# Two routings of a mixture-of-experts kernel: first router's operands swapped, stores ahead of weights, bf16 tables relaid, lots of 18, 8 and 6 tiles

## The reference, cut to what matters

```
x: 16 sequences x 256 tokens x 128; 8 experts; hidden size 512
x = x + 0.5 * ffn(layernorm(x))
x = x + attention(layernorm(x))        # 16 heads of 8; q, k: rms norm, then rope
x = x + 0.5 * ffn(layernorm(x))        # the same weights

ffn(z): e = argmax(z @ Wr.T + br)      # one expert per token
        y = relu(z @ W1[e].T + b1[e]) @ W2[e].T + b2[e]
```

## Time and profile before

| | us |
|---|---|
| median of 3 runs | 552.09 (551.03 to 552.29) |
| profiled execution | 550.08 |
| its span, first to last instruction | 547.6 |
| PE / DVE / ACT / POOL busy | 477.7 / 385.6 / 339.2 / 288.6 |

### The profile page before, as it was taken

How to read it: one execution, slowest core, us unless ns; L and a number is a source line. 1 busy time by engine, 2 the same in 40 slices (tenths; PEclk the granted TensorE clock), 3 DMA queues, 4 the chain that set the end, 5 groups by cost and what they waited for, 6 DMA issues and landing times.

```text
span 547.6 us, 13826 instructions
## 1 busy us (share of the span) xinstructions
PE 477.7 (87%) x4184; PEld 344.8 (63%) x4187; DVE 385.6 (70%) x1044; ACT 339.2 (62%) x763; POOL 288.6 (53%) x407
## 2 busy tenths in 40 slices
PE   6958999999688899999999999998988269979991
PEld 6825999996244555555555555555554159869991
DVE  6194777773578688888988888878886048956760
ACT  2204667661353688888888888887766436546650
POOL 6005455432699577777675656664037704564442
PEclk9998999999895699999999999999997869998997
DMA  8971222211000000000000000000001122223100
GB/s 226 344 129 37 59 64 67 68 37 40 26 25 11 20 12 13 13 7 13 8 12 7 2 2 5 2 3 2 2 23 56 54 49 78 75 65 86 46 30 0
DMA packets 28566, 24.88 MB, mean 45 GB/s; under 512 B 5651, under 2 KB 26042, under 8 KB 28240
## 3 DMA queue, kind: packets, MB, share of 16 engines
q1 hardware_dynamic: 23952, 15.52, 10.6%
q0 software_dynamic: 4544, 8.49, 5.5%
HBM read 14.65 MB, written 9.99 MB: 45 GB/s over the span
## 4 chain that ended last, share of the span: by engine, by line
PE 65%; DVE 14%; issue 9%; ACT 4%; DMA 3%; POOL 2%; DVEq 1%; POOLq 0%; ACTq 0%; SPq 0%
PE PS L647 12%; PE PS L660 11%; PE PS L786 10%; PE PS L749 9%; DVE Smax L1422 6%; PE PS L734 5%; PE PS L719 4%; PE PS L596 2%; PE PS L771 2%; PE PS L816 2%; PE PS L796 1%; ACT QkT L871 1%; PE PS L589 1%; PE PS L637 1%; PE PS L759 1%
## 5 line engine op out<-in xcount | busy, mean ns | idle before, releaser
L1422 DVE TENSOR_REDUCE Smax<-PS 128x4 f32<-128x1024 f32 x128 | 156.1, 1223 | 39.5 <-PE PS L749 37.2
L967 ACT ACTIVATE Pt<-PS 128x1024 f32<-128x1024 f32 x128 | 128.4, 1033 | 4.8 <-PE PS L771 4.0
L647 PE MATMUL PS<-XsT,Ws 128*128 128x128 f32 x624 | 91.6, 291 | 2.0 <-ACT XsT L871 2.0
L660 PE MATMUL PS<-W,HsT 128*128 x624 | 84.8, 279 | 3.8 <-DVE Ys L1320 2.7
L910 ACT ACTIVATE HsT<-PS,Bs 128x128 f32<-128x128 f32 x156 | 48.7, 363 | 63.1 <-PE PS L647 57.9
L647 PEld LDWEIGHTS PS<-XsT,Ws 128*128 128x128 f32 x624 | 78.0, 196 | 7.2 <-ACT XsT L871 3.2
L660 PEld LDWEIGHTS PS<-W,HsT 128*128 128x128 f32 x624 | 76.9, 194 | 6.6 <-issue 6.4
L439 POOL DMA_INDIRECT Xs<-rows,TokI x39 | 39.1, 1001 | 70.0 <-DVE TokI L1275 34.9
L749 PE MATMUL PS<-QkT 24*128 24x256 f32 x512 | 64.5, 329 | 12.9 <-DVE Smax L1422 9.4
L749 PEld LDWEIGHTS PS<-QkT 24*128 24x128 f32 x512 | 40.8, 192 | 49.6 <-issue 17.8
L786 PE MATMUL PS<-Pt,Vg 128*32 128x256 f32 x1024 | 71.0, 396 | 0.1
(11 more groups left out here) (183 smaller groups left out, 735.2 us busy)
## 6 DMA issues: line engine op xcount, KB each, us to landing
AtCol<-slots SPq DMA_DIRECT2D x39, 65.5 KB, 1.8
mid<-Ys SPq DMA_DIRECT2D x39, 64.0 KB, 1.6
rows<-XX SPq DMA_DIRECT2D x8, 260.0 KB, 8.8
XX<-x SPq DMA_DIRECT2D x8, 256.0 KB, 4.5
W<-w1T SPq DMA_DIRECT2D x1, 2048.0 KB, 8.2
W<-w2T SPq DMA_DIRECT2D x1, 2048.0 KB, 13.1
QkT<-NmaxT SPq DMA_DIRECT2D x64, 4.0 KB
Xs<-rows,TokI POOLq DMA_INDIRECT x39
```

Source lines behind the costliest of these rows:

```text
L647: last = nc.tensor.matmul(PS[:, 2 + 2 * (n % 2) + c // 2, (c % 2) * P:(c % 2 + 1) * P], Ws[:, n % R_WS, c * P:(c + 1) * P], XsT[:, n % 2, ...
L660: last = nc.tensor.matmul(PS[:, y_bank(n), 0:P], HsT[:, n % 2, c, :], W2[:, ds(e * D_FF + c * P, P)], start=(c == 0), stop=(c == FC - 1))
L967: nc.scalar.activation(Pt[:, m % 2, 2 * pair:2 * pair + 2, :, :].rearrange("p h c t -> p (h c t)"), PS[:, score_bank(m, pair):score_bank(m ...
L1422: nc.vector.tensor_reduce(Smax[:, b % 2, :, at:at + 33:32].rearrange("p t h -> p h t"), PS[:, max_bank(m, pair):max_bank(m, pair) + 2, :]. ...
```

## The change

Router 1: `Wr32`, the centred weights in 32 columns, is now stationary and `XT` moves, 512 tokens at a time; four groups go to four strips of 32 partitions of one bank, ACT copies it (`logits_copy`), and PE turns it back (`turn_logits`). `XT` keeps all 8 groups, and all of them can be turned with three banks. PE starts with 8 filler matmuls. Row stores move ahead of W2, B2 and the attention weights on SP, with the wait for `ln_shift`; the semaphore `w_in` is split in three. The tables have the tile number innermost, their operands are bf16, and `ColAll` and `TileAll`, written by POOL, hold their counting side in full. `AtCol` is one operation, and `invert` starts behind it. B2's scaling stands behind `TokI`. Routing 2: lots of 18, 8 and 6 tiles instead of 16, 10 and 6, lot 0 in steps 47 to 51 instead of 52 to 55.

```diff
-ROUTE_LOTS = ((0, 16), (16, 26), (26, 32))
-POOL_NORM_AT = 44
+ROUTE_LOTS = ((0, 18), (18, 26), (26, 32))
+POOL_NORM_AT = 42
...
-HOT_AT = {52: 0, 57: 1}
+HOT_AT = {47: 0, 57: 1}
...
-PLACE_AT = {55: 0, 59: 1}
+PLACE_AT = {51: 0, 59: 1}
...
-        ModF = sb("ModF", [P, N_TILES])
+        ModF = sb("ModF", [P, N_TILES], BF16)
-        AtCol = sb("AtCol", [P, N_TILES, P], BF16)
-        AtTile = sb("AtTile", [P, N_TILES, S_TILES], BF16)
-        Ids = sb("Ids", [P, N_TILES, 2, S_TILES], BF16)
+        AtCol = sb("AtCol", [P, P, N_TILES], BF16)
+        AtTile = sb("AtTile", [P, S_TILES, N_TILES], BF16)
+        Ids = sb("Ids", [P, 2, S_TILES, N_TILES], BF16)
...
+        XT = Pt[:].rearrange("p u h c t -> p (u h c t)").rearrange("p (c x) -> p c x", c=N_CHUNK)
...
-        XT = Sq[:].rearrange("p u q t d -> p u (q t d)")
+        LgT = Sq[:].rearrange("p u q t d -> p u (q t d)")
...
+        ColAll = RotRn[:].rearrange("p a u q t d -> p (a u q t d)").bitcast(BF16).rearrange("p (c j) -> p c j", j=N_TILES)
...
+        TileAll = YuT[:].rearrange("p g t -> p (g t)").bitcast(BF16)[:, 0:S_TILES * N_TILES].rearrange("p (t j) -> p t j", j=N_TILES)
...
+        TURN_BANKS, LGT_BANKS, LG_BANKS = (0, 1, 4), (2, 3), (6, 5)
...
-            for dst, src in ((W1, w1T), (W2, w2T), (B2, b2.partition_broadcast(P)),
-                             (G8, g_rms.partition_broadcast(P)), (Cos, rope_cos), (Sin, rope_sin)):
-                sp.dma_start(dst[:], src).then_inc(w_in, 16)
...
+            sp.dma_start(W1[:], w1T).then_inc(w1_in, 16)
+            sp.wait_ge(ln_shift, 1)
+            for c in range(N_CHUNK):
+                a, b = c * CH, (c + 1) * CH
+                sp.dma_start(row_tiles[:, a:b, :], XX[:, a:b, 0:P + 2]).then_inc(rows_out[c], 16)
+            for dst, src in ((W2, w2T), (B2, b2.partition_broadcast(P))):
+                sp.dma_start(dst[:], src).then_inc(w2_in, 16)
+            for dst, src in ((G8, g_rms.partition_broadcast(P)), (Cos, rope_cos), (Sin, rope_sin)):
+                sp.dma_start(dst[:], src).then_inc(rope_in, 16)
...
                     sp.dma_start(Wp[at:at + HD, 0:P], wpT[HD * (GH * g + h):HD * (GH * g + h + 1), :]).then_inc(wp_in, 16)
-
-            sp.wait_ge(ln_shift, 1)
-            for c in range(N_CHUNK):
-                a, b = c * CH, (c + 1) * CH
-                sp.dma_start(row_tiles[:, a:b, :], XX[:, a:b, 0:P + 2]).then_inc(rows_out[c], 16)
...
-            nc.gpsimd.iota(TileCol[:], [[1, S_TILES]], channel_multiplier=0, allow_small_or_imprecise_dtypes=True).then_inc(const_done, 1)
+            nc.gpsimd.iota(TileAll, [[1, S_TILES], [0, N_TILES]], channel_multiplier=0, allow_small_or_imprecise_dtypes=True).then_inc(const_done, 1)
+            nc.gpsimd.iota(ColAll, [[1, P], [0, N_TILES]], channel_multiplier=0, allow_small_or_imprecise_dtypes=True).then_inc(const_done, 1)
...
-            def turn_chunk(c, bank):
+            def turn_chunk(c):
+                pe.wait_ge(x_in[c], 16)
+                if c >= len(TURN_BANKS):
+                    pe.wait_ge(xnT_ready, c - len(TURN_BANKS) + 1)
                 for u in range(CH):
-                    last = nc.tensor.transpose(PS[:, bank, u * P:(u + 1) * P], X[:, CH * c + u, :], I[:])
+                    last = nc.tensor.transpose(PS[:, TURN_BANKS[c % len(TURN_BANKS)], u * P:(u + 1) * P], X[:, CH * c + u, :], I[:])
                 last.then_inc(xnT_ps, 1)
 
-            def logits(c, bank):
-                pe.wait_ge(xnT_ready, c + 1)
+            def logits(r):
+
+                pe.wait_ge(xnT_ready, CH * (r + 1))
+                for i in range(CH):
+                    last = nc.tensor.matmul(PS[32 * i:32 * i + 32, LGT_BANKS[r], :], Wr32[:], XT[:, CH * r + i, :],
+                                            start=True, stop=True)
+                last.then_inc(lgT_ps, 1)
+
+            def turn_logits(r):
+                pe.wait_ge(lgT_ready, r + 1)
                 for u in range(CH):
-                    j = CH * c + u
-                    last = nc.tensor.matmul(PS[:, bank, j * N_EXP:(j + 1) * N_EXP],
-                                            XT[:, c % 2, u * P:(u + 1) * P], WrC,
-                                            start=True, stop=True)
+                    last = nc.tensor.transpose(PS[:, LG_BANKS[r], u * P:(u + 1) * P], LgT[:, r, u * P:(u + 1) * P], I[:])
                 last.then_inc(logits_ps, 1)
...
                 pe.wait_ge(ids_ready, 2)
+                pe.wait_ge(at_col, 1)
                 for j in range(N_TILES):
-                    if j % (N_TILES // 2) == 0:
-                        pe.wait_ge(at_col, 2 * j // N_TILES + 1)
-                    last = nc.tensor.matmul(PS[:, 3, 0:2 * S_TILES], AtCol[:, j, :],
-                                            Ids[:, j, :, :].rearrange("p a t -> p (a t)"),
+                    last = nc.tensor.matmul(PS[:, 3, 0:2 * S_TILES], AtCol[:, :, j],
+                                            Ids[:, :, :, j].rearrange("p a t -> p (a t)"),
                                             start=(j == 0), stop=(j == N_TILES - 1))
...
+            pe.wait_ge(const_done, 1)
+            fill_const(8)
             pe.wait_ge(turn_in, 16 * 2)
             pe.wait_ge(unit_ready, 1)
             nc.tensor.matmul(PS[:, 5, 0:N_EXP], Unit[:], Wr[:], start=True, stop=True).then_inc(wr_sum, 1)
-            pe.wait_ge(const_done, 1)
-            for c in range(N_CHUNK + 1):
-                if c < N_CHUNK:
-                    pe.wait_ge(x_in[c], 16)
-                    if c >= 2:
-                        pe.wait_ge(xnT_ready, c - 1)
-                    turn_chunk(c, c % 2)
-                if c == 1:
-                    pe.wait_ge(wr_centred, 1)
-                if c >= 1:
-                    logits(c - 1, 2)
+            for c in range(6):
+                turn_chunk(c)
+                if c < 4:
+                    fill_const(1)
+            pe.wait_ge(wr_centred, 1)
+            logits(0)
+            turn_chunk(6)
+            turn_chunk(7)
+            turn_logits(0)
+            logits(1)
...
-            fill_const(8)
+            turn_logits(1)
+            fill_const(14)
             totals()
-            fill_const(20)
+            fill_const(22)
             invert()
-            fill_const(14)
-            pe.wait_ge(w_in, 16 * 8)
+            fill_const(18)
+            pe.wait_ge(w2_in, 16 * 2)
             experts(0)
...
-                    nc.tensor.matmul(PS[:, 5, :], AtCol[:, 0, :], AtCol[:, 0:4, :].rearrange("p j d -> p (j d)"),
+                    nc.tensor.matmul(PS[:, 5, :], Col[:], Col[:].unsqueeze(1).to_broadcast([P, 4, P]),
...
-            for c in range(N_CHUNK):
-                if c == N_CHUNK // 2:
-                    inverse_deviation(0)
-                chunk_copy(c, c % 2)
+            for c in range(6):
+                chunk_copy(c)
+            logits_copy(0)
+            for c in range(6, N_CHUNK):
+                chunk_copy(c)
+            logits_copy(1)
+            inverse_deviation(0)
...
-                dve.wait_ge(logits_ps, N_CHUNK)
+                for r in range(2):
+                    half = slice(r * N_TILES // 2, (r + 1) * N_TILES // 2)
+                    dve.wait_ge(logits_ps, r + 1)
+                    last = tt_(Lg[:, half].rearrange("p (i u) e -> p u i e", u=CH),
+                               PS[:, LG_BANKS[r], :].rearrange("p (u i x) -> p u i x", u=CH, i=CH)[:, :, :, 0:N_EXP],
+                               Rstd[:, half].rearrange("p (i u) -> p u i", u=CH).unsqueeze(3).to_broadcast([P, CH, CH, N_EXP]),
+                               ALU.mult)
                 dve.wait_ge(route_in, 16 * 5)
-                scaled_logits(every, PS[:, 2, 0:N_TILES * N_EXP].rearrange("p (j e) -> p j e", e=N_EXP))
+                link(last)
+                link(tt_(Lg[:], Lg[:], Br[:].unsqueeze(1).to_broadcast([P, N_TILES, N_EXP]), ALU.add))
...
-                wide = [P, N_TILES, S_TILES]
-                tt_(AtTile[:], TileCol[:].unsqueeze(1).to_broadcast(wide),
-                    DivF[:].unsqueeze(2).to_broadcast(wide), ALU.is_equal).then_inc(at_tile, 1)
+                wide = [P, S_TILES, N_TILES]
+                tt_(AtTile[:], TileAll, DivF[:].unsqueeze(1).to_broadcast(wide), ALU.is_equal).then_inc(at_tile, 1)
                 dve.wait_ge(at_tile, 1)
-                tt_(Ids[:, :, 0, :], AtTile[:], FromEnd[:].unsqueeze(2).to_broadcast(wide), ALU.mult).then_inc(ids_ready, 1)
-                for a in range(0, N_TILES, N_TILES // 2):
-                    b = a + N_TILES // 2
-                    wide = [P, N_TILES // 2, P]
-                    tt_(AtCol[:, a:b, :], Col[:].unsqueeze(1).to_broadcast(wide),
-                        ModF[:, a:b].unsqueeze(2).to_broadcast(wide), ALU.is_equal).then_inc(at_col, 1)
+                tt_(Ids[:, 0, :, :], AtTile[:], FromEnd[:].unsqueeze(1).to_broadcast(wide), ALU.mult).then_inc(ids_ready, 1)
```

(17 more changed lines are left out.)

47 lines of the change are left out of this document (27 added, 20 removed).

## The result

On the chip of the first comparison the kernel after took 544.5 us (median of 11 runs, 541.4 to 559.7) and the kernel before beside it 552.3: 0.986 of it, 95% interval 0.983 to 0.989. That is 7.8 us faster, where I had forecast 22.6; 544.5 lies above my range. The profiled execution took 547.41 us, span 545.6.

The account below looks back on a forecast made before the run. Bounds: the router (0 to 47 us; PE, then DVE alone) and 11.00 us of issue between attention and second experts. Router -11.4 and second routing -11.2 made -22.6: profiled 550.08 to 527.5, median 529.5 us; range 521 to 539.

Parts of the forecast that it names:

- Logit group: Router, sign to look for: PE's logit group takes 1.1 us, not 1.9.
- the rival of a clock that never rises: Router: PE stays at half clock, +5.8 us, 535.3 in all; chance 0.20.
- AtTile 0.81 and AtCol 2.29: Router tables: bf16, innermost-dense operands bring AtTile near 0.8 and AtCol near 2.3; tables together -3.4 us.
- the second half of the router's product: Router: DVE's product, now two halves, ends at 16.1 instead of 25.40, -9.3 us.
- the seam's arithmetic: Between attention and second expert stage: last store issued by 426.6, first Xr at 430.9 instead of 441.27, -10.4 us.
- DVE's routing work of lot 0: Second routing: 4.0 us of work moved into attention steps 47 to 51 lengthens attention by +1.2 us.
- W2 and B2 at 404 GB/s: Router loads: queued behind row stores ending at 27.2, they land at 33.7, in time for Xr; +0.5 us booked.
- 32 matmuls behind it instead of 16: Router inversion: waiting for the whole AtCol costs +1.2 us, ends 0.6 and 3.6.
- the lesser case: Router rival: 64-byte steps make the inversion cost double, +2.4 us; chance 0.10 together with tables not speeding up.
- After the idle 11 us: Start of second expert stage: without idle time PE keeps full clock, -2 us, ends 0 and -2.5.
- the router's 11.4: Router's summed gain at the first Xr: -9.3 - 3.4 + 1.2 - 0.4 + 0.5 = -11.4 us.
- 11.2: Second routing's summed gain: seam -10.4, DVE work +1.2, clock -2, together -11.2 us.

Follow-up runs that it names:

- scans_first: Kernel after with lot 0's scans at the head of step 49, ahead of the normalisation: 537.8 us, 0.976 of the kernel before.
- warm: scans_first with 36 instead of 22 filler matmuls ahead of the inversion and 40 instead of 18 behind: 571.3 us (0.998); on another chip 565.0 (0.994).
- tiles_outer: scans_first with the first routing's tables in the old layout, tiles outermost and columns contiguous: 574.4 us, 1.008 of the kernel before.
- parts 2 to 5: Follow-up experiments on four other chips, with variants of the kernels before and after; the kernel before took 569.7, 567.7, 566.8 and 570.1 us there.

## Why the prediction was wrong

**Right.** Logit group 1.07 (forecast 1.1), so the rival of a clock that never rises is out; AtTile 0.81 and AtCol 2.29 (0.80, 2.28); the second half of the router's product ended at 16.10 (16.1), in part by luck, since its norm's factors came at 15.64 for 14.7; the seam's arithmetic, as scans_first shows (9.7 of 10.4).

**Wrong, in the order of size.**
- *"DVE's routing work of lot 0 ... between no cost and 4.0 I take +1.2".* This is the step that failed. It was about 6.5 in the changed kernel: attention ended 8.8 us late, of which 2.3 came in from its start, and the lateness grows from 2.3 to 11.5 in steps 48 to 52. I counted VectorE's microseconds and did not ask what GpSimd does in step 49: beside its split the scans take 3.69 us for 0.89, PE waits 2.94 for them, and its clock falls to 0.50. scans_first gives back 5.3 us by the ratios (0.986 to 0.976).
- *"W2 and B2 at 404 GB/s take 6.5 more: 33.7 ... I book +0.5 (ends 0, +3)".* The overlap failed here. B2's scaling ended at 39.67, and from the token list to the first Xr it took 8.9 us, not 4.2, so that in effect +5.2 stood where I had booked +0.5: outside my ends. The rows' stores filled the DMA engines at 145 to 179 GB/s until about 30, not 27.2; then the weights ran at 354, not far from my 404, and W2, issued at 23.40, landed at about 37.0. The gather, issued at 34.65 behind them, landed 7.81 us later, where the first gather of the kernel before took 2.56. I booked the transfers one by one and did not ask how long a gather takes behind the weights, nor that with the weights first it would wait for the rows.
- *"32 matmuls behind it instead of 16 ... +1.2".* It was 3.6, the end that I had named for each taking twice as long. The Trainium skill's rule, "SBUF — State Buffer", "Door 1: The DMA port swizzle", which I had held to be the lesser case, pointed the right way, and warm beside tiles_outer agrees. None of it reached Xr.
- *Not booked:* the first experts start at half clock, 2.08 us for each of their first two groups where warm has 1.16; it costs 1.8.
- *"After the idle 11 us ... -2".* Not gained: after 2.38 us of issue the first group took 2.08 again.

So of the router's 11.4, 4.3 were there at the first Xr, 2.5 to 2.9 at the end of the experts in most traces (0.85 in the changed kernel's own) and 3.5 in the medians; the second routing gave about 4.3 of 11.2 (0.994 to 0.986). On the chips of parts 2 to 5 the standstill behind the stores decides, which the trace that I predicted from did not show.
